# Graph network on one core: the nodes of each item are turned for the next layer inside the item pipeline, instead of in rounds between the layers

## The reference

```python
xl = (x @ Wl + bl).reshape(n, heads, outc)
e_feat = leaky_relu(xl[src] + (x @ Wr + br).reshape(n, heads, outc)[dst], 0.2)
logits = einsum('ehc,hc->eh', e_feat, att)
m = segment_max(logits, dst)
a = exp(logits - m[dst])
a = a / segment_sum(a, dst)[dst]
out = segment_sum(xl[src] * a[:, :, None], dst) + bias
# between the layers
h = relu(_ln(out, g, be))        # layer norm over the 128 features of a node
# after the third layer
x = _layernorm(x + h)
x = _layernorm(x + mlp_with_batch_norm(x, mean_of_edge_attributes, u))
```

## Time and profile before

| | us |
|---|---|
| median of 3 runs | 8319.16 (8298.82 to 8323.32) |
| the profiled execution's own time | 8224.01 |
| its span in the profile | 8221.9 |
| first gather of layer 0 starts | 142.16 |
| last gather of layer 0 / first of layer 1 starts | 2735.16 / 2884.11 |
| last gather of layer 1 / first of layer 2 starts | 5354.04 / 5498.43 |
| last gather of layer 2 starts | 7961.52 |

### The profile page before, as it was taken

How to read it: one execution, slowest core, us unless ns; L and a number is a source line. 1 busy time by engine, 2 the same in 40 slices (tenths; PEclk the granted TensorE clock), 3 DMA queues, 4 the chain that set the end, 5 groups by cost and what they waited for, 6 DMA issues and landing times.

```text
span 8221.9 us, 103854 instructions
## 1 busy us (share of the span) xinstructions
PE 5220.3 (63%) x25358; PEld 4292.5 (52%) x25358; DVE 4814.5 (59%) x13989; ACT 4364.0 (53%) x10671; POOL 4777.4 (58%) x4843
## 2 busy tenths in 40 slices
PE   5676676777766755665666666666565665566656
PEld 2666666666656444554555555434444554445444
DVE  3555555555555655655666656655666665666656
ACT  2555455555555455555555555545555555555546
POOL 1666666666666166666666666616666666666640
PEclk7777777777777666666666666656666666666666
DMA  4333323333333422222222222242222222222221
GB/s 122 85 85 84 84 79 84 86 85 84 85 85 85 88 54 53 54 53 54 55 54 54 54 54 54 54 86 54 54 54 54 54 54 54 54 54 54 54 53 47
DMA packets 402713, 544.76 MB, mean 66 GB/s; under 512 B 124846, under 2 KB 310244, under 8 KB 394734
## 3 DMA queue, kind: packets, MB, share of 16 engines
q0 software_dynamic: 154752, 327.15, 17.8%
q1 hardware_dynamic: 247917, 217.13, 9.5%
HBM read 490.62 MB, written 53.26 MB: 66 GB/s over the span
## 4 chain that ended last, share of the span: by engine, by line
POOL 50%; issue 32%; DMA 10%; PE 4%; DVE 2%; ACT 1%; POOLq 1%; SPq 0%; DVEq 0%; ACTq 0%
POOL xl_g L643 50%; DMA xl_g<-xl_tab,edges 9%; PE PS L676 2%; PE PS L795 1%; PE PS L675 1%; DVE ea L1071 0%; PE PS L729 0%; POOLq L638 0%; POOLq L641 0%; ACT n_hT L831 0%; DMA state<-n_new 0%; ACT msg L950 0%; DMA digit_tab<-S 0%; DMA ea<-state 0%; POOLq L633 0%
## 5 line engine op out<-in xcount | busy, mean ns | idle before, releaser
L643 POOL DMA_INDIRECT xl_g<-xl_tab,edges x4836 | 4776.6, 988 | 3184.8 <-issue 2738.8
L1140 DVE TENSOR_TENSOR z<-PS,xl_g 128x528 f32<-128x528 f32 x1302 | 868.8, 667 | 2786.2 <-DMA xl_g<-xl_tab,edges 2226.0
L729 PE MATMUL PS<-msg,S 128*128 128x137 f32 x9672 | 1844.6, 360 | 1011.3 <-DVE msg L1239 772.6
L729 PEld LDWEIGHTS PS<-msg,S 128*128 128x128 f32 x9672 | 1680.5, 256 | 1173.9 <-issue 1059.5
L703 PE MATMUL PS<-xr_w,ST 128*128 128x132 f32 x9672 | 1929.7, 360 | 61.5 <-DVE z L1140 44.5
L875 ACT ACTIVATE distT<-PS,neg_node 128x512 f32<-128x512 f32 x1302 | 843.1, 648 | 1934.3 <-PE PS L693 787.7
L703 PEld LDWEIGHTS PS<-xr_w,ST 128*128 128x128 f32 x9672 | 1747.2, 265 | 200.5 <-issue 170.3
L852 ACT ACTIVATE dist<-node_row,neg_dst 128x128 f32<-128x128 f32 x4836 | 1534.6, 386 | 0.0
L693 PE MATMUL PS<-digits,digit_w 2*128 2x512 bf16 x1302 | 598.0, 459 | 1276.7 <-ACT distT L875 794.0
L693 PEld LDWEIGHTS PS<-digits,digit_w 2*128 2x128 bf16 x1302 | 122.6, 94 | 1570.4 <-ACT distT L875 907.8
L1147 DVE SCALAR_TENSOR_TENSOR am<-z,att_relu 128x512 f32<-128x512 f32 x1302 | 854.8, 657 | 6.4
(11 more groups left out here) (200 smaller groups left out, 3278.6 us busy)
## 6 DMA issues: line engine op xcount, KB each, us to landing
xl_g<-xl_tab,edges POOLq DMA_INDIRECT x4836
ea<-edge_attr SPq DMA_DIRECT2D x62, 1248.0 KB
xr_w<-xr_tab SPq DMA_DIRECT2D x186, 66.0 KB
dst_r<-dst_rows SPq DMA_DIRECT2D x186, 64.0 KB
node_row<-node_id SPq DMA_DIRECT2D x186, 64.0 KB
xl_tab<-xl_g SPq DMA_DIRECT2D x30, 330.0 KB, 3.7
xr_tab<-xl_g SPq DMA_DIRECT2D x30, 330.0 KB, 5.2
st_old<-state SPq DMA_DIRECT2D x124, 68.0 KB
```

What stands on the lines that cost most here:

```text
L643: pool.indirect_dma_start(xl_g[:, q, t, :], None, xl_tab[:, :], bass.IndirectOffsetOnAxis(idx[:, q, t:t + 1], 0))\
L729: last = pe.matmul(agg_ps, S[:, q, t, :], msg[:, t, :], start=t == 0, stop=t == TILES - 1)
L1140: dve.tensor_tensor(out=z[:, (q + g) % 2, 0:n, :], in0=zp[(q + g) % 2][:, 0:n, :], in1=xl_g[:, q, a:a + n, :], op=ALU.add).then_inc(z_done ...
```

## The change

The rounds between layers 0 and 1 and between 1 and 2 are removed. Instead each step of the pipeline has a fourth item, `turned`, one behind the item that is closed. At the end of the step that closes an item, DVE normalizes the 128 rows of its window straight from `st_new` (`turn_norm`: bn_stats for mean and variance, and the root by an integer estimate and three Newton steps, so that ACT isn't needed). In the following step PE transposes and multiplies them, ACT applies scale, bias and relu and copies the products out, DVE computes the self-loop logits, and SP stores 128 rows each of the next layer's `xl_tab`, `xr_tab` and `state`. Windows overlap: rows whose edges were not complete are written again by the next item. The three tables now exist once per layer. At the end of a layer one more step turns the last item, and POOL waits for the last store of the next `xl_tab` only. The setup cuts the windows so that they leave out no node, and fills the last 256 rows of the new tables. The rounds before layer 0 stay. After layer 2 the perceptron's rounds load a row's first 136 numbers from the table of layer 2 and the other 97 from that of layer 0, in two DMAs instead of one.

The core of the diff:

```diff
+        xl_tab = [scratch(f"xl_tab{l}", (N_PAD, XW)) for l in range(LAYERS)]
+        xr_tab = [scratch(f"xr_tab{l}", (N_PAD, XW)) for l in range(LAYERS)]
+        state = [scratch(f"state{l}", (N_PAD, ROW if l == 0 else ROW_L)) for l in range(LAYERS)]
...
+            def turned(i, q):
+                return item(i, q) if stage < LAYERS - 1 else None
+            step(None, None, item(0, 0), None)
+            step(item(0, 0), None, item(0, 1), None)
+            step(item(0, 1), item(0, 0), item(1, 0), None)
+            step(item(1, 0), item(0, 1), item(1, 1), turned(0, 0))
+            with eng.Fori(1, last_pair) as i:
+                step(item(i, 1), item(i, 0), item(i + 1, 0), turned(i - 1, 1))
+                step(item(i + 1, 0), item(i, 1), item(i + 1, 1), turned(i, 0))
+            step(item(last_pair, 1), item(last_pair, 0), None, turned(last_pair - 1, 1))
+            step(None, item(last_pair, 1), None, turned(last_pair, 0))
+            if stage < LAYERS - 1:
+                step(None, None, None, turned(last_pair, 1))
...
+            for at in (N_PAD - 2 * P, N_PAD - P):
+                sp.dma_start(state[LAYERS - 1][at:at + P, :], t_new[:, :]).then_inc(table_out, 16)
+                for l in range(1, LAYERS):
+                    sp.dma_start(xl_tab[l][at:at + P, :], t_new[:, 0:XW]).then_inc(table_out, 16)
+            sp.wait_ge(table_out, 112)
...
+                    sp.dma_start(n_st[q][:, :, 0:ROW_L], rounds_of(state[LAYERS - 1], r)).then_inc(st_loaded[q], 16)
+                    sp.dma_start(n_st[q][:, :, ROW_L:ROW], rounds_of(state[0], r)[:, :, ROW_L:ROW]).then_inc(st_loaded[q], 16)
...
+            def store_turned(k, stage, before):
+                base = window(k)
+                sp.wait_ge(n_copied, before + k + (ROUNDS + 1))
+                sp.dma_start(xl_tab[stage + 1][bass.ds(base, P), :], t_lr[:, 0, :]).then_inc(turn_xl, 16)
+                sp.dma_start(xr_tab[stage + 1][bass.ds(base, P), :], t_lr[:, 1, :]).then_inc(turn_rest, 16)
+                sp.wait_ge(n_made, before + k + (ROUNDS + 1))
+                sp.sem_inc(spacer, 1)
+                sp.wait_ge(n_first, before + k + (ROUNDS + 1))
+                sp.dma_start(state[stage + 1][bass.ds(base, P), :], t_new[:, :]).then_inc(turn_rest, 16)
...
+                def item_step(k, q, behind):
+                    here, ahead = window(k), window(k + 1)
+                    sp.wait_ge(onehot_done[NG - 1], (before + k + 1) * 2)
+                    sp.sem_inc(spacer, 1)
+                    sp.wait_ge(logit_done[NG - 1], (before + k + 1) * 3)
+                    sp.sem_inc(spacer, 1)
+                    load_item(k + 2, q, stage)
+                    if turns and behind:
+                        store_turned(k - 1, stage, before)
+                    sp.wait_ge(item_done, before + k + 1)
+                    sp.dma_start(state[stage][bass.ds(here, P), :], st_new[:, q, 0:ROW if first else ROW_L]).then_inc(state_stored, 16)
+                    if first:
+                        load_attributes(k + 2, q)
+                    sp.wait_ge(state_stored, (before + k + 1) * 16)
+                    sp.dma_start(st_old[:, 1 - q, 0:ROW if first else ROW_L], state[stage][bass.ds(ahead, P), :]).then_inc(state_loaded[1 - q], 16)
...
+                if turns:
+                    store_turned(k, stage, before)
+                sp.wait_ge(state_stored, (before + k + 1) * 16)
...
+                if stage == 0:
+                    for q in range(2):
+                        pool.wait_ge(n_stored[q], stored_value * (ROUNDS // 2 + 1))
+                else:
+                    pool.wait_ge(turn_xl, pairs * (2 * stage * 16) + 16)
...
+                    def turn_rows():
+                        q, v, use = turned
+                        pe.wait_ge(turn_normed, v)
+                        pe.transpose(t_hT_ps, t_norm[:, :], ident[:, :]).then_inc(n_T, 1)
+                    def turn_products():
+                        q, v, use = turned
+                        pe.wait_ge(n_Tc, v + ROUNDS)
+                        pe.matmul(t_lr_ps, ones_h[:, :], b_parts[:, stage + 1, :, :].rearrange("a s f -> a (s f)"), start=True, stop=False)
+                        pe.matmul(t_lr_ps, t_hT[:, :], w_lr[:, stage + 1, :, :].rearrange("p s f -> p (s f)"), start=False, stop=True)\
+                            .then_inc(n_prod, 1)
...
+                        if g == 0 and turned:
+                            pe.wait_ge(n_copied, turned[1] + ROUNDS)
...
+                            if turned:
+                                turn_rows()
...
+                    def turn_hidden():
+                        q, v, use = turned
+                        act.wait_ge(n_T, v + ROUNDS)
+                        act.activation(t_hT[:, :], t_hT_ps, ACT.Relu, bias=be_col[:, stage:stage + 1], scale=g_col[:, stage:stage + 1]).then_inc(n_Tc, 1)
+                    def turn_copies():
+                        q, v, use = turned
+                        act.wait_ge(n_prod, v + ROUNDS)
+                        act.wait_ge(turn_xl, v * 16)
+                        act.sem_inc(spacer, 1)
+                        act.wait_ge(turn_rest, v * 32)
+                        act.copy(t_lr[:, :, :].rearrange("p s f -> p (s f)"), t_lr_ps).then_inc(n_copied, 1)
+                        act.wait_ge(n_copied, v + ROUNDS)
+                        act.copy(t_new[:, C_ACC:C_ACC + F], t_lr[:, 0, 0:F]).then_inc(n_first, 1)
...
+                def turn_norm():
+                    q, v, use = closes
+                    n = Chain(dve, logit_step, v * TURN_STEPS + (ROUNDS * LOGIT_STEPS - TURN_STEPS))
+                    dve.wait_ge(item_done, v)
+                    n.link(dve.reciprocal(t_rd[:, :], st_new[:, q, C_DEN:C_DEN + HEADS]))
+                    n.link(dve.tensor_tensor(out=t_y[:, :].rearrange("p (h f) -> p h f", h=HEADS),
+                                             in0=st_new[:, q, C_ACC:C_ACC + F].rearrange("p (h f) -> p h f", h=HEADS),
+                                             in1=t_rd[:, :].unsqueeze(2).to_broadcast([P, HEADS, F // HEADS]), op=ALU.mult))
+                    n.link(dve.tensor_tensor(out=t_y[:, :], in0=t_y[:, :], in1=c_b[:, stage, :], op=ALU.add))
+                    dve.sem_inc(spacer, 1)
+                    n.link(dve.bn_stats(t_bn[:, :], t_y[:, :]))
+                    dve.sem_inc(spacer, 1)
+                    n.link(dve.bn_aggr(t_mv[:, :], t_bn[:, :]))
+                    n.link(dve.tensor_scalar(t_var[:, :], t_mv[:, 1:2], EPS, None, ALU.add))
+                    dve.tensor_scalar(t_half[:, :], t_var[:, :], -0.5, None, ALU.mult)
+                    n.link(dve.tensor_scalar(t_bits[:, :], t_var[:, :].bitcast(I32), 1, None, ALU.arith_shift_right))
+                    n.link(dve.tensor_scalar(t_rstd[:, :].bitcast(I32), t_bits[:, :], -1.0, RSQRT_BITS, ALU.mult, ALU.add))
+                    for _ in range(3):
+                        n.link(dve.scalar_tensor_tensor(t_newton[:, :], t_rstd[:, :], t_half[:, 0:1], t_rstd[:, :], ALU.mult, ALU.mult))
+                        n.link(dve.scalar_tensor_tensor(t_rstd[:, :], t_newton[:, :], 1.5, t_rstd[:, :], ALU.add, ALU.mult))
+                    dve.tensor_scalar(t_norm[:, :], t_y[:, :], t_mv[:, 0:1], t_rstd[:, 0:1], ALU.subtract, ALU.mult).then_inc(turn_normed, 1)
...
+                def turn_logits():
+                    q, v, use = turned
+                    n = Chain(dve, logit_step, v * TURN_STEPS + (ROUNDS * LOGIT_STEPS - 4))
+                    dve.wait_ge(n_copied, v + ROUNDS)
+                    n.link(dve.tensor_tensor(out=t_sum[:, :], in0=t_lr[:, 0, 0:F], in1=t_lr[:, 1, 0:F], op=ALU.add))
+                    n.link(dve.scalar_tensor_tensor(t_relu[:, :], t_sum[:, :], 0.0, att_relu[:, stage + 1, :], ALU.max, ALU.mult))
+                    if stage + 1 < LAYERS - 1:
+                        n.link(dve.reduce_sum(t_rs[:, :], t_relu[:, :].rearrange("p (h f) -> p h f", h=HEADS), axis=AX.X))
...
+                    dve.tensor_tensor(out=t_new[:, 0:HEADS], in0=t_m[:, :], in1=t_lr[:, 1, F:XW], op=ALU.add).then_inc(n_made, 1)
...
+                    if turned and g == 2:
+                        turn_logits()
...
+                    if stage < LAYERS - 1:
+                        turn_norm()
...
-            def node_step(stage):
-                def step(ahead, behind):
-                    if ahead:
-                        n = layer_mean(stage - 1, ahead)
-                    if behind:
-                        loop_logits(stage, behind)
-                    if ahead:
-                        layer_norm(n, stage - 1, ahead)
-                return step
```

265 lines of the change are left out of this document (133 added, 132 removed).

## The result

The changed kernel took 8095.3 us (median of 4 runs, 8086.9 to 8123.3), the kernel before 8309.0 beside it (8294.0 to 8323.3): ratio 0.9749, 95% interval 0.9717 to 0.9781, 214 us faster. The forecast was 8156 and 163 us, with 8108 as its low end. The direction was right, the size wrong: the measured median lies under the low end.

What follows compares the result with a forecast made beforehand. POOL's chain of gathers was taken to set the pace. Terms of -215 + 31 + 8 + 3 + 10 = -163 us, taken from 8319, gave 8156 us, with a range of 8108 to 8215 (8125 to 8190 at 0.60).

Steps and rivals of the forecast that it cites:

- stores: Layers 0 and 1: three turned stores an item collide with gathers, 0.25 us an item, 31 us (0 to 110).
- longer gathers: Layers 0 and 1: new DVE instructions lengthen POOL's gathers by at most 0.1 us an item, 8 us (0 to 25).
- perceptron's load: Perceptron rounds after layer 2: two DMAs of short rows replace one, costing 10 us (0 to 25).
- attribute load: Layer 0: existing 1248 KB load costs 2.0 us an item, 1.6 us per MB; used to price the stores.
- pauses: Two layer ends: POOL's idle of 147.7 and 143.1 us falls to 39.0 and 36.5, gaining 215 us.
- DVE, SP, PE, ACT in the layers: Layers 0 and 1: added work, 4.9 us an item on DVE, is covered by idle time and costs nothing.
- setup: Before layer 0: six more stores issued ahead of loading `tab` delay everything behind it by 3 us.
- the drain and the last turn: Layer ends: new pause is a drain of 24.2 or 21.7 us plus 4.9, then a serial last turn of 9.9.
- one rival: Layers and perceptron rounds: collisions cost nothing and the perceptron's load stays hidden, -208 us, 8111 us; chance 0.20.
- The wait of 1 to 2 us for `state`: Perceptron's rounds: the profile after would show them waiting 1 to 2 us for `state`.
- Layers 0 and 1 each +20: First to last gather start grows by some 20 us in layers 0 and 1 each, in layer 2 not at all.
- The forecast's own test: Prediction is wrong if layers 0 and 1 stretch by over 60 us each, or a pause is over 50.

Runs made afterwards that it cites:

- experiment 1: Kernel before and changed kernel, both unchanged, run again: 8243.3 against 8039.8 us, ratio 0.9757; profiled executions 8235 and 8037.
- first pair: First profiles of the kernel before (execution of 8224.0 us, median 8309.0) and of the changed kernel (execution of 8123.3, median 8095.3); ratio 0.9749.
- 2: Changed kernel with the three turned stores issued twice, 8072.0 us, or cut to one row each, 8019.7 us.
- 3: Changed kernel with the chain of turn_norm computed twice for each item: 8078.9 us, 28 us over the changed kernel.
- pinned pair: Kernel before and changed kernel, each with layer 0's attribute load issued only at the change to group 2: 8142.9 and 7924.9 us.
- experiment 4, `norm_l2`: Changed kernel with turn_norm run in layer 2 as well, its result unused there: 8052.3 us against 8065.1 for the changed kernel.
- 6: Kernel before with the attribute load issued only at the change to group 2: 8142.9 us, ratio 0.9903; unchanged changed kernel beside it 8065.1, ratio 0.9808.
- 7: Changed kernel with the setup's six stores moved behind the load of the item table, 8045.3 us; with the perceptron's state loaded in one DMA, 8048.5 us.
- 5: Changed kernel with the attribute load issued at the change to group 2, 7924.9 us; in five pieces behind third landings, 7886.2; five pieces without waits, 7929.5.
- `a3_again`: Changed kernel, unchanged, run again in a later comparison: 8065.1 us, ratio 0.9808 to the kernel before.
- `best`: Changed kernel with the attribute load in five pieces and the turned stores behind third landings, and setup's stores off the chain: 7846.1 us, ratio 0.9548.
- `b_again`: Kernel before, unchanged, run again for a second profile: 8243.3 us (9 runs).
- `a_again`: Changed kernel, unchanged, run again: 8039.8 us, ratio 0.9757 to the kernel before.
- the pin: Layer 0's attribute load issued only when the third gather of group 1 has landed: changed kernel 7924.9 us, kernel before 8142.9.
- `nostore`: Changed kernel with each turned store cut to one row, layers 1 and 2 using layer 0's tables: 8019.7 us, ratio 0.971 to the kernel before.
- second pair: Profiles of kernel before and changed kernel, both unchanged, from their second comparison: executions 8235 and 8037 us, medians 8243.3 and 8039.8.

## Why the prediction was wrong

The steps that failed are terms of the sum. For layers 0 and 1 the forecast had +39 us (stores +31, longer gathers +8); in the pair of experiment 1 it is +6 (idle +23, gathers -17). For the perceptron's load it had +10, and the tail grew by 1. And the attribute load had no term, though the change moves its cost from one comparison to the next. Forecast against measured:

| term | forecast | measured | from |
|---|---|---|---|
| pauses | -215 | -209 (first pair -214) | 1 |
| stores | +31 | +31, +32; all idle added in layers 0 and 1 in one pair +23 | 2, 1 |
| DVE, SP, PE, ACT in the layers | 0 | 0 | 3 |
| gathers' length | +8 | -17 (first pair -18, pinned pair -25); -14 for `turn_norm` alone in one layer | 1, 4, 6 |
| setup | +3 | +4; first gather not resolved (+14 in one pair) | 7, 1 |
| perceptron's load | +10 | 0 to 1 | 7 |
| layer 2 | 0 | -10, and +27 in the first pair | 1 |
| attribute load | not in the sum | pinned pair -218, unpinned ones -161 to -214 | 5, 6 |

The two profiles of experiment 1 differ by 198 us, 35 more than the forecast. Of these, 33 lie in layers 0 and 1, 9 in the tail and 10 in layer 2; the first gather (11) and the pauses (6) went the other way. So the mechanism of the gain, the drain and the last turn, was right to a microsecond in the first profile, and what was taken off again was too much. That layer 2 and the first gather nearly cancel is luck.

**The gathers' length had the wrong sign.** The step read the earlier trace rows rightly: a gather takes 1.46 us where `am` starts just before it. But it only asked whether the new instructions are long enough to do the same, with a rule (a wait grows with the square of the length) that no run shows. What counts more is where they push the old ones: `z` and `am` of the first two groups come up to 4 us later and meet fewer gathers (experiment 4). That is 17 us in the pair of experiment 1, against 8 us of loss in the forecast. That `turn_norm` does it is shown; how far it goes is not fixed: POOL's busy time in layer 1 fell from 1594 to 1583 there, but it is 1595 in `a3_again` and 1580 in `best`.

The Trainium skill, SBUF — State Buffer, on who interferes with whom, has VectorE instructions with two SBUF inputs contend with a GpSimd instruction that reads SBUF. The earlier trace rows and the gathers of over 1.1 us agree that they meet; but by that rule alone more such work would lengthen the gathers, and POOL's 1592 us became 1579.

**The perceptron's load was hidden**, as one rival said. The earlier trace rows shows a wait of 0.36 us in front of an operation, and the step took all that the new load costs as added to that wait. In the changed kernel that wait is 0.37. Of the ten loads only the first is waited for longer; in `b_again` and in `a_again`:

```profile
8002.73 0.28 DVE L1079 RECIPROCAL n_rd<-ea 128x20 f32<-128x20 f32 x1 [6.08 <-DMA ea<-state]
```

```profile
7805.73 0.28 DVE L1169 RECIPROCAL n_rd<-ea 128x20 f32<-128x20 f32 x1 [9.73 <-DMA ea<-state]
```

The other loads had slack, which one row with a small wait didn't show. The tail from the last gather to the end is 1 us longer in this pair.

**The price of the attribute load was taken as a price per byte** (1.6 us per MB). For the stores that happened to hold, which is luck. The load's own cost is a matter of its place: with the pin, 131 us go in layer 0 of the changed kernel and 59 in that of the kernel before. The pinned pair differs by 218 us, the unpinned one beside them by 161: unpinned, the turn makes the load dearer. The forecast had no such term. That it does so by moving the load is not shown. Where the load comes 6.7 to 7.0 us behind the item's first gather, change 2 idles 3.5 to 3.6 us in three profiles of the kernel before and 3.7 to 4.7 in four of the changed one, and 3.9 in `nostore`, so neither that place nor the stores explain the difference; why is open.

**One profile stood for all executions.** The gain itself was 214, 203, 205 and 161 us in four comparisons whose intervals are +-11 to 27 us each; the kernel before had medians of 8225 to 8309. So a forecast of 163 was met once and missed three times. The 95% interval of one comparison doesn't hold the next one, and the range (48 us below the forecast, 59 above) was made of terms only. What differs between comparisons isn't settled. Some profiles show DVE 5 to 20 us late in some items of layer 0, where the attribute load is then issued at another place. And the profiles of the two comparisons with 8225 show another rhythm even in layer 2, which no edit but `norm_l2`'s touches: the first `z` of a step waits 0.3 us there and change 3 idles 1.36 to 1.40, in all others 1.5 to 2.5 us and 1.44 to 1.63.

The signs that were named: the pauses came nearly as foretold in the first pair (40.0 and 36.5 us for 36 to 39; in the second pair the first was 44.4, with DVE late in the last items of layer 0), and so did DVE's idle (the idle before its additions went from 16.1 to 10.3 us an item in layer 0 and from 14.0 to 7.9 in layer 1, some 6 us instead of 5) and the near zero wait before the first `z` (0.05 us in layer 0, 0.26 in layer 1). The wait of 1 to 2 us for `state` did not come. "Layers 0 and 1 each +20" failed: +18 and -12 in the pair of experiment 1, +71 and -3 in the first. The forecast's own test asked for both layers to stretch by over 60 us; in the first pair layer 0 alone did, and no other profile repeats it. The nearest rival in time (collisions cost nothing and the load is hidden, 8111 us) had one mechanism right and one wrong: the collisions cost 31 us, which the shorter gathers hid in part. The longer loops didn't fetch their program anew: 64 fetches in all of the changed kernel, 44 before, with some 30 passes over two items in each layer.

## What to carry to other kernels

A transfer beside this paced stream of gathers had no price per byte. Find the moment at which the stream starts to have slack (here the landing of the third gather of a group) and issue it there, in pieces that fit; that was worth 168 us of a layer of 2638, nearly as much as the whole change. When work is added to an engine with idle time, ask not only whether it fits but what it shifts, since the instructions behind it meet the other engines at other moments afterwards. Before a gain of 2% is forecast, compare two executions of the same kernel by layer: what moves between them (here the layer with the big load, by 15 to 50 us) belongs into the range.

## What was not expected of the hardware

- 16 more instructions an item on VectorE made GpSimd's 1612 gathers of a layer 14 us shorter in all (1592 to 1579).
- 0.24 MB issued right behind the landing of a third gather cost nothing that can be seen where no store went with it (idle 1.2 to 1.4 us at the next change); 1.2 MB issued there cost 1.0 us, and 2 to 3.7 us where they were issued during the first gathers of a group.
- With one landing less to wait for, this kernel ran 29% slower, though each gather was no longer (976 ns against 987).
